# A perceiver block on one core: the operands of the first two stages kept in single precision

## The reference

```python
ln_out = _ln(hidden_states, ln_w, ln_b)            # x: (16, 64, 256)
q = _fp8_linear_pertensor(ln_out, wq, ...)         # rounds ln_out / scale to fp8, then a matmul
q = _ln(q, ...); k = _ln(fp8_linear(wk)); v = fp8_linear(wv)      # 16 heads, 8 groups, 128 wide
core = _gqa(q, k, v)                               # self-attention over 64 tokens
qx = _ln(fp8_linear(wqx))
kvx = jnp.einsum('bsi,oi->bso', cond, w_kv_x)      # cond = ctx_2048: (16, 1601, 256)
kx, vx = jnp.split(kvx, 2, axis=-1); kx = _ln(kx, ...)
xout = _gqa(qx, kx, vx)                            # cross-attention over 1601 rows
catq = _div_clamp_fp8(concatenate([core, xout]), proj_smooth)     # fp8 again
return jnp.einsum('bsi,oi->bso', catq, wproj) * (proj_in_scale * proj_w_scale)
```

## Time and profile before

| | |
|---|---|
| time, median of 3 runs | 2800.32 us (2798.15 to 2800.42) |
| time of the profiled execution | 2799.96 us |
| its span | 2798.2 us |
| PE busy | 2278.0 us (81%) |
| PEld busy | 1812.5 us (65%) |
| DVE busy | 2104.4 us (75%) |
| ACT busy | 1554.5 us (56%) |
| POOL busy | 1571.4 us (56%) |
| mean granted clock | 0.921 |

### The profile page before, as it was taken

How to read it: one execution, slowest core, us unless ns; L and a number is a source line. 1 busy time by engine, 2 the same in 40 slices (tenths; PEclk the granted TensorE clock), 3 DMA queues, 4 the chain that set the end, 5 groups by cost and what they waited for, 6 DMA issues and landing times. The chain is left out here.

```text
span 2798.2 us, 50477 instructions
## 1 busy us (share of the span) xinstructions
PE 2278.0 (81%) x18514; PEld 1812.5 (65%) x18514; DVE 2104.4 (75%) x4502; ACT 1554.5 (56%) x3129; POOL 1571.4 (56%) x1619
## 2 busy tenths in 40 slices
PE   2466662699999999999999999999999999855556
PEld 1243441578877877877877877877877878644334
DVE  8888885477787778778787787778778787558763
ACT  4455451566666666666666666666666667411211
POOL 2465655766766766767666766766767655340000
PEclk8687875999999999999999999999999999977778
DMA  2001103110010010110110111010010100073100
GB/s 105 16 29 40 46 23 115 55 38 31 26 50 32 25 44 34 31 44 32 32 38 31 34 43 32 32 44 26 31 52 25 32 9 1 1 271 96 40 12 8
DMA packets 74482, 119.45 MB, mean 43 GB/s; under 512 B 21168, under 2 KB 56576, under 8 KB 73216
## 3 DMA queue, kind: packets, MB, share of 16 engines
q1 hardware_dynamic: 74240, 116.23, 12.3%
HBM read 94.20 MB, written 22.02 MB: 42 GB/s over the span
## 5 line engine op out<-in xcount | busy, mean ns | idle before, releaser
L71 PE MATMUL x_kc<-x_wk,x_ctxT 128*128 128x256 f16 x4992 | 622.8, 274 | 52.8 <-POOL x_ctxT L975 40.0
L997 POOL TENSOR_TENSOR x_kT<-x_kf,x_kT 128x512 f16<-128x512 f32 (+1 forms) x448 | 629.6, 1405 | 37.3
L71 PE MATMUL x_ox<-x_ctxp,x_pt 128*128 128x256 f16 x4992 | 619.0, 273 | 0.0
L995 POOL TENSOR_SCALAR x_kT<-x_kf 128x512 f16<-128x512 f32 (+1 forms) x448 | 288.2, 643 | 583.8 <-ACT x_kf L1067 581.8
L71 PEld LDWEIGHTS x_kc<-x_wk,x_ctxT 128*128 128x128 f16 x4992 | 481.6, 98 | 131.6 <-issue 40.2
L71 PEld LDWEIGHTS x_ox<-x_ctxp,x_pt 128*128 128x128 f16 x4992 | 486.3, 98 | 70.1 <-DVE x_on L1328 14.0
L1055 ACT ACTIVATE x_kraw<-x_kc 128x512 f32<-128x512 f32 (+1 forms) x448 | 254.3, 568 | 426.3 <-PE x_kc L71 214.5
L1263 DVE TENSOR_REDUCE x_ss<-x_sq 128x4 f32<-128x512 f32 (+1 forms) x448 | 283.1, 642 | 230.5 <-ACT x_sq L1059 228.9
L1320 DVE TENSOR_TENSOR x_pt<-x_tp,x_pt 128x512 f16<-128x512 f32 (+1 forms) x512 | 297.4, 584 | 117.5 <-ACT x_pt L1094 113.7
L1067 ACT ACTIVATE x_kf<-x_tp,x_hv 128x512 f32<-128x512 f32 (+1 forms) x448 | 330.7, 755 | 76.5 <-PE x_tp L1146 72.7
L1181 PE MATMUL x_tp<-x_ident,x_pb 128*128 128x128 f32 x1664 | 256.5, 274 | 52.8 <-ACT x_pb L1088 50.6
(11 more groups left out here) (234 smaller groups left out, 3181.5 us busy)
## 6 DMA issues: line engine op xcount, KB each, us to landing
x_stage<-in_ctxT SPq DMA_DIRECT2D x32, 800.5 KB, 4.3
x_stage<-in_ctx SPq DMA_DIRECT2D x16, 896.0 KB, 5.1
x_stage<-in_ctx SPq DMA_DIRECT2D x16, 640.0 KB
scr_q<-a_qxT SPq DMA_DIRECT2D x8, 1024.0 KB, 3.9
x_qs<-scr_q SPq DMA_DIRECT2D x16, 512.0 KB, 5.4
scr_core<-a_catc SPq DMA_DIRECT2D x8, 512.0 KB, 2.6
scr_x<-x_catx SPq DMA_DIRECT2D x8, 512.0 KB, 2.6
f_area<-in_wprojT SPq DMA_DIRECT2D x4, 1024.0 KB, 11.4
```

The lines of the kernel that those rows point to most:

```text
L71: last = pe.matmul(out, lhs[i], rhs[j], start=start and n == 0, stop=stop and n == len(parts) - 1)
L995: gp.tensor_scalar(dst[0], src, 1.0, 0.0, ALU.mult, ALU.add).then_inc(khi_ready, 1)
L997: gp.tensor_tensor(dst[1], src, dst[0], ALU.subtract).then_inc(kT_ready, 1)
```

## The change

All operands of matmuls in the first two functions are kept as one f32 tile instead of two f16 tiles, and each product is one `pe.matmul`. With that go: `split_heads`, `split_v`, `low_weights`, the `lo` of the probabilities, `convert_piece`, `split_unit`, and the buffers `tf`, `stage`, `kf`, `wst`. Weights and contexts are loaded by DMA straight into the tiles that TensorE reads; ACT writes turned heads and keys straight into `qT`, `qxT`, `kT`. POOL has only `ident`, `xq` and `keep_core` left in the first function and only `ident` in the second. The context loads of the second function are issued per batch, when `pv_done` or `kc_filled` says that the slot is free. The orders of PE and ACT stay; `DVE_ORDER` loses its "pt" and "oa" entries. `finish` is not changed. The factor 256 on the weights (`WSCALE`) goes. The diff, cut to its core:

```diff
-        wp = sb("wp", [P, 2, KC, 6144], F16)
-        wst_own = sb("wst", [P, 2, KC, 1024])
+        wp = sb("wp", [P, KC, 6144])
...
+            for n, (name, c) in enumerate((("wqT", 0), ("wqT", 1), ("wqxT", 0), ("wqxT", 1), ("wkT", 0), ("wvT", 0))):
+                sp.dma_start(wp[:, :, n * 1024:(n + 1) * 1024],
+                             a[name].rearrange("(k p) n -> p k n", p=P)[:, :, c * 1024:(c + 1) * 1024]
+                             ).then_inc(w_ready[n], 16)
...
-            def split_heads(T):
-                first = isinstance(T, int) and T == 0
-                for u in range(HU):
-                    gp.wait_ge(tf_ready, T * HU + u + 1)
-                    if u == 0 and not first:
-                        wait_filled(gp, T - 1, ("s", 1))
-                    if u == 4 and not first:
-                        gp.wait_ge(q_stored, T * 16)
-                    gp.sem_inc(passed, 1)
-                    src = tf[:, u % 2].rearrange("p (h b s) -> p h b s", h=4, b=BT)
-                    hi, lo = unit_dst(u, 0), unit_dst(u, 1)
-                    gp.tensor_scalar(hi, src, 1.0, 0.0, ALU.mult, ALU.add).then_inc(pool, 1)
-                    gp.wait_ge(pool, T * HU + u + 1)
-                    gp.tensor_tensor(lo, src, hi, ALU.subtract).then_inc(parts_ready, 1)
 
...
-            def high_weights(n):
+            def scaled_weights(n):
                 m = [0, 0, 1, 1, 2, 3][n]
-                act.wait_ge(wst_ready[n % 4], 16 * (n // 4 + 1))
+                act.wait_ge(w_ready[n], 16)
                 for k in range(KC):
-                    act.activation(wp[:, 0, k, n * 1024:(n + 1) * 1024], wst[n % 4][:, k], ACT.Copy,
-                                   scale=vec[:, k, 2 + m:3 + m]).then_inc(whi_ready, 1)
+                    w = wp[:, k, n * 1024:(n + 1) * 1024]
+                    act.activation(w, w, ACT.Copy, scale=vec[:, k, 2 + m:3 + m]).then_inc(wp_ready, 1)
...
-                if u >= 2 or not (isinstance(t, int) and t < 0):
-                    act.wait_ge(parts_ready, (t + 1) * HU + u - 1)
+                if 4 <= u < 8 and not (isinstance(t, int) and t < 0):
+                    act.wait_ge(q_stored, (t + 1) * 16)
                 col = unit_heads(u)[3]
                 bank = u % 4 if isinstance(t, int) and t < 0 else bank_of(("t", u))
-                act.activation(tf[:, u % 2], tr[:, bank], ACT.Identity, scale=hv[:, col:col + 1],
-                               bias=hv[:, 4 + col:5 + col]).then_inc(tf_ready, 1)
...
-                    last = products(pe, pr[:, proj_bank(T, bank)], [xq[:, m, k, bass.ds(T * P, P)]],
-                                    [wp[:, i, k, bank * 512:(bank + 1) * 512] for i in range(2)],
-                                    k == 0, k == KC - 1, EXACT_LEFT)
+                    last = pe.matmul(pr[:, proj_bank(T, bank)], xq[:, m, k, T * P:(T + 1) * P],
+                                     wp[:, k, bank * 512:(bank + 1) * 512], start=k == 0, stop=k == KC - 1)
...
-                        last = products(pe, tr[:, bank, i * S:(i + 1) * S],
-                                        [qT[:, n, b, g * P:(g + 1) * P] for n in range(2)],
-                                        [kT[:, n, b, g, :] for n in range(2)], True, True)
+                        last = pe.matmul(tr[:, bank, i * S:(i + 1) * S], qT[:, b, g * P:(g + 1) * P], kT[:, b, g, :],
+                                         start=True, stop=True)
...
-            def low_weights(n0, n1):
-                for n in range(n0, n1):
-                    m = [0, 0, 1, 1, 2, 3][n]
-                    v.wait_ge(wst_ready[n % 4], 16 * (n // 4 + 1))
-                    v.wait_ge(whi_ready, KC * (n + 1))
-                    for k in range(KC):
-                        ins = v.scalar_tensor_tensor(wp[:, 1, k, n * 1024:(n + 1) * 1024], wst[n % 4][:, k],
-                                                     vec[:, k, 2 + m:3 + m], wp[:, 0, k, n * 1024:(n + 1) * 1024],
-                                                     ALU.mult, ALU.subtract)
-                    ins.then_inc(wlo_ready, 1)
...
-        wk = sb("wk", [P, 2, KC, G * D], F16)
-        wv = sb("wv", [P, 2, KC, G * D], F16)
-        stage = sb("stage", [P, 2, 7 * C])
-        ctxT = sb("ctxT", [P, 2, 2, KC, LP], F16)
-        ctxp = sb("ctxp", [P, 2, 2, CH, C], F16)
+        wk = sb("wk", [P, KC, G * D])
+        wv = sb("wv", [P, KC, G * D])
+        ctxT = sb("ctxT", [P, 2, KC, LP])
+        ctxp = sb("ctxp", [P, 2, CH, C])
...
+            def load_rows(b):
+                slot = b % 2
+                src = a["ctx"][b]
+                for lo, hi in ((0, 6), (6, 12)):
+                    sp.dma_start(ctxp[:, slot, lo:hi, :], src[lo * P:hi * P, :].rearrange("(c p) n -> p c n", p=P)
+                                 ).then_inc(ctx_ready[slot], 16)
+                if b < 2:
+                    sp.wait_ge(pads_ready, 6)
...
+                    if jj == 1 and b >= 1 and b + 1 < B:
+                        sp.wait_ge(pv_done, b * 8)
+                        load_rows(b + 1)
+                    if jj == 2 and b + 2 < B:
+                        sp.wait_ge(kc_filled, (b + 1) * SPB * KU)
+                        load_features(b + 2)
...
-            def split_unit(JK, j, i):
-                cs = chunks(i)
-                n = len(cs) * P
-                gp.wait_ge(kf_ready, JK * KU + i + 1)
-                if i == 0 and not (isinstance(JK, int) and JK < 2):
-                    gp.wait_ge(sc_done, (JK - 1) * 2)
-                met()
-                src = kf[:, (j * KU + i) % 4, 0:2 * n].rearrange("p (g n) -> p g n", g=2)
-                dst = [kT[:, j % 2, p, :, cs[0] * P:cs[0] * P + n] for p in range(2)]
-                gp.tensor_scalar(dst[0], src, 1.0, 0.0, ALU.mult, ALU.add).then_inc(khi_ready, 1)
-                gp.wait_ge(khi_ready, JK * KU + i + 1)
-                gp.tensor_tensor(dst[1], src, dst[0], ALU.subtract).then_inc(kT_ready, 1)
...
-                if not (isinstance(JK, int) and u < 4):
-                    act.wait_ge(kT_ready, u - 3)
-                act.activation(kf[:, (jk * KU + i) % 4, 0:n], tp[:, bank, 0:n], ACT.Identity, scale=hv[:, 3:4],
-                               bias=hv[:, 7:8]).then_inc(kf_ready, 1)
+                if i == 0 and JK >= 2:
+                    act.wait_ge(sc_done, (JK - 1) * 2)
+                act.activation(kT[:, jk % 2, :, cs[0] * P:cs[0] * P + n],
+                               tp[:, bank, 0:2 * n].rearrange("p (g n) -> p g n", g=2), ACT.Identity,
...
-                        ins = products(pe, kc[:, n * 256:(n + 1) * 256],
-                                       [ctxT[:, slot, p, k, c * P:(c + 1) * P] for p in range(2)],
-                                       [wk[:, p, k, gp_ * 256:(gp_ + 1) * 256] for p in range(2)], k == 0, k == KC - 1)
+                        ins = pe.matmul(kc[:, n * 256:(n + 1) * 256], ctxT[:, slot, k, c * P:(c + 1) * P],
+                                        wk[:, k, gp_ * 256:(gp_ + 1) * 256], start=k == 0, stop=k == KC - 1)
...
-                        ins = products(pe, out, [qs[:, b, p, g * P:(g + 1) * P] for p in range(2)],
-                                       [kT[:, j % 2, p, A_, n * 512:n * 512 + w] for p in range(2)], True, True)
+                        ins = pe.matmul(out, qs[:, b, g * P:(g + 1) * P], kT[:, j % 2, A_, n * 512:n * 512 + w],
+                                        start=True, stop=True)
...
-                        ins = products(pe, ox[:, 0:C], [pt[:, A_, p, c * P:(c + 1) * P] for p in range(2)],
-                                       [ctxp[:, slot, p, c, :] for p in range(2)], c == 0, c == CH - 1)
+                        ins = pe.matmul(ox[:, 0:C], pt[:, A_, c * P:(c + 1) * P], ctxp[:, slot, c, :],
+                                        start=c == 0, stop=c == CH - 1)
...
-                    n = min(4, CH - 4 * i) * P
-                    v.wait_ge(pthi_ready, (J * 2 + A_) * 4 + i + 1)
-                    v.tensor_tensor(pt[:, A_, 1, i * 512:i * 512 + n], tp[:, tp_bank(j, o), 0:n],
-                                    pt[:, A_, 0, i * 512:i * 512 + n], ALU.subtract).then_inc(ptlo_ready, 1)
...
```

More of the change, by code:

```diff
@@ L385, in evacuate @@
                 else:
[L386 to L387 removed]
+                    act.activation(vv[:, (bank - HU) * 512:(bank - HU + 1) * 512], src, ACT.Copy,
+                                   scale=wsc[:, 3:4]).then_inc(vv_ready, 1)
             def normalise(T):
@@ L432, in _ @@
                 evacuate(0, bank)
[L433 removed]
+            scaled_weights(4)
             scaled_input(2)
@@ L515, in fill @@
                 else:
-                    pe.wait_ge(vlo_ready, t * 2 + 2)
-                    pe.wait_ge(ptlo_ready, t * 4 + j + 1)
+                    pe.wait_ge(vv_ready, t * 2 + 2)
+                    pe.wait_ge(pt_ready, t * 4 + j + 1)
                     for i in range(4):
                         g = 2 * j + i // 2
-                        last = products(pe, tr[:, bank, i * P:(i + 1) * P],
```

(45 more changed lines are left out.)

286 lines of the change are left out of this document (92 added, 194 removed), and 8 rows, old and new, of the table DVE_ORDER.

## The result

The changed kernel takes 3110.63 us (median of four runs, 3109.88 to 3112.38) against 2800.35 for the kernel before on the same chip: 1.111 times as long, 95% interval 1.1092 to 1.1130. 3128 was predicted, within 3070 to 3230. The profiled execution took 3110.64 us, its span 3108.8.

A forecast was written before the change was run, and what follows sets the result against it. TensorE was taken to bound the second function's steps, DVE as nearest bound in the first function's tiles. 2799.96 + 454 (dearer products) - 100 (idle time) - 7 (second function's start) - 18 (first function) = 3129, given as 3128; range 3070 to 3230.

The forecast's parts named there:

- Idle time: Second function's steps: 100 of PE's 109.8 us idle time go, through longer products and the missing `lo` waits.
- Small products: Small f32 products in the steps: two instructions of 0.11 us, 0.22 at 65 columns; +18 ("sr") and +15 ("ob").
- Start of the second function: First projection 13 us earlier, less 5.4 or somewhat more for dearer products ahead of the steps: net -7.
- the first `kc` at some 13 us after its weights arrive: A sign that would show the forecast right: timing of the first `kc` after its weights.
- First function: Opening -12, tiles -3, before the last tile -4, first turn of heads +1: sum -18 us.
- The opening: Start of the first function: DVE loses 23.2 us of `low_weights`, half of the gain is left, -12.
- The tiles: First function: -0.5 us a tile, -3 in all.
- the -4 before the last tile: First function: DVE's 6.28 us for the `lo` heads go, against 2 us more in the projection of v.
- The feared drop to 1.2 GHz: Rival: PE stays at 1.2 GHz in the first function, +139 us, 3267, or half of it, 3197; chance 0.05.
- half price: Rival: a f32 product is one instruction of 0.215 us at 256 columns, giving about 2390 us; chance 0.04.
- Exposed loads: Rival: weight loads add 6552 instructions x 0.19 = +1245 us more; chance 0.01.
- That the idle time stays: Rival: f32 may only shift the steps' hand-overs, 2799.96 + 454 - 25 = 3229 us; chance 0.08.

The follow-up runs named there:

- run 2: Kernel before, with a fourth f16 matmul (lo x lo) in every product of the second function: 3161.5 us, ratio 1.1295.
- run 3: Changed kernel, with each product of the second function made of three f16 matmuls on a fixed tile: 2685.6 us, ratio 0.9598.
- run 4: Changed kernel, with each key product (out `kc`) cut into two f32 products of 128 columns: 3130.4 us, ratio 1.1185.
- run 5: Changed kernel, with every unit of turned heads in the first function passed over GpSimd through two buffers: 3149.5 us, ratio 1.1243.
- run 10: Changed kernel, with every unit of turned heads in the first function passed over GpSimd through five buffers: 3141.1 us, ratio 1.1222.
- run 7: Changed kernel, with the operands of all products of the second function as float32r: 2362.5 us, ratio 0.8434.
- run 9: Changed kernel with float32r operands in the second function and the squares of the keys moved from ACT to GpSimd: 2376.3 us, ratio 0.8487.

## Why the prediction was right, and where it was off

| Step | predicted | measured |
|---|---|---|
| f32 product, 256 columns | 0.430 us, two instructions | 0.430, x3328 |
| one step | 35.5 us | 35.55 in the middle (1405.66 to 1441.21), 35.3 on the mean of 64 |
| steps, work less idle time | +454 - 100 = +354 | +345.2 |
| PE in the steps | 97% or more, clock 1.00 | 98.9%, 1.00 |
| start of the second function | -7 | -7.6 |
| first function | -18 | -28.6 |
| from there to the end | 0 | +1.7 |

*Price and mechanism.* The price read from `finish` held at shapes that before didn't have. The sum was right because PE bounded the steps and its clock stood at 1.00 on both sides.

*Idle time.* 85.8 of the 109.8 us went by the rows, not 100: 19.1 remain in the wait for the exponentials, where the sum had left some 10 for everything. Runs 2 and 3 show that the mechanism for it was the one named, the length of the work; for the `lo` waits, which the prediction gave to the removal of the parts, the length alone would have done as well.

*Small products.* The 65-column product takes 0.17 us (1409.37 to 1409.54 in run 4), not 0.22: 6 us less over 128. With 85.8 for 100 and these 6 the steps would cost some 362, so about 17 us are missing from the rows. Most of them are time that the rows hide in each wait. First a wait of PE in before, then the same group with no wait behind it:

```profile
1408.08 0.50 PE L71 MATMUL x_tp<-x_onT,x_wv 128*128 128x128 f16 x6
1409.36 0.63 PE L1181 MATMUL x_tp<-x_ident,x_pb 128*128 128x128 f32 x4 [0.79 <-ACT x_pb L1088]
...
1455.49 0.50 PE L71 MATMUL x_tp<-x_onT,x_wv 128*128 128x128 f16 x6
1455.82 0.39 PE L1146 MATMUL x_tp<-x_ident,x_kn 128*128 128x128 f32 x2
```

From start to start the group takes 1.28 us with the wait and 0.33 without: 0.95 are lost where the row says 0.79, since the modelled end of the last matmul counts as busy. The steps have 154 listed waits in before and 72 in after; 82 x 0.16 = 13 us. Counted from start to start, then, the idle time fell by some 99 us, and the -100 came out nearly right; it was set as a share of the listed 109.8, so that is partly luck. Some 4 us stay open.

*Start of the second function.* The first projection begins 12.0 us after the function is entered (431.34 to 443.34), 25.6 in before: a gain of 13.6, of which the dearer products ahead of the steps take 6.0 back. Both terms were right. The sign "the first `kc` at some 13 us after its weights arrive" was not: DVE's last wait for weights ends at 437.81, 5.5 us before the projection.

*First function.* Here the step failed by size: -18 for -28.6. The opening was near (-12 and +1 for the first turn; first scores 13.3 earlier, not the 12.3 that run 5's expectation has). The tiles gave 6.7 in place of 3, the last tile took 5.5 more, which I hadn't counted, and the -4 before the last tile ("DVE's 6.28 for the `lo` heads go, against 2 us more in the projection of v") should have been -14 (43.0 to 28.8 us from one tile's scores to the next). The earlier trace rows show DVE waiting 6.28 there, but PE's own row of the same moment, in the trace of before, says for whom DVE waited in the end:

```profile
428.81 1.38 PE L71 MATMUL a_tr<-a_kT,a_qT 128*128 128x64 f16 x23 [10.82 <-POOL a_kT L329]
```

This was the row to read; runs 5 and 10 show the place, the chain of GpSimd's ten units. In the tiles the prediction also counted only DVE's `lo` operations: DVE is busy 41.7 us less in six tiles (230.4 to 188.7), and only 23 of them are `lo`; the rest lies in instructions that were longer beside GpSimd's work, such as `a_pp` and `a_yf`. The feared drop to 1.2 GHz went the other way: 0.90 for 0.76.

*Rivals.* One instruction a product is what float32r has (run 7), not f32, and it costs 0.12 us, not the 0.215 of "half price". That kernel 7 lands at 2362, near the 2390 given for that rival, is therefore no test of it: products at nearly half of its price ended only 28 us lower, because far more idle time came back (370 us of 1400) than the 60 it allowed. Exposed loads are excluded by run 4 and by after's price itself. That the idle time stays is excluded by after's 24.0 us and by run 2.

## What to carry to other kernels

Count a f32 product of 128 to 512 columns as two instructions, each at half the f16 rate: here it costs a third more than three f16 passes over split operands. It saves the splitting, which here was worth some 113 us (run 3) against 454 of added work. Where an engine bounds a stretch at full clock, the added work is the added time, less the waits that it grows long enough to cover; count those from start to start, since each listed wait hides 0.16 us more. And look at the last hand-over of a chain, not at the engine's mean load: GpSimd, busy 58% of the first function's stretch, held PE up for 10.82 us before the last tile, where DVE's own row named PE.

## What was not expected of the hardware

- f32 weight loads of 0.19 us (0.098 for f16, in before) run at one every 0.112 us (run 4), so they overlap.
- Some DVE instructions are longer in the kernels in which GpSimd splits heads: `a_pp` 0.745 us in run 5 against 0.422 in after, `a_yf` 2.17 against 1.23.
- float32r products take one instruction of about 0.12 us at 256 columns, against 0.109 for f16 and 0.430 for f32.
- The granted clock in the first function rose with more work for PE, 0.76 to 0.90, and in the steps it fell in the float32r kernels, where PE rests more often (0.94 and 0.89 in runs 7 and 9, 1.00 in after).
